# Channel attention on one core: streams of 64 columns, a fourth buffer of rows, and another order on TensorE

## The reference, cut to what matters

```python
q, k, v = xs @ Wq.T, xs @ Wk.T, 2 * (xs @ Wv.T)         # xs: normed rows, 3136 tokens an image, 128 channels
q, k, v_h = l2norm of q, k, v by head                   # 8 heads of 16 channels
attn_head = softmax(einsum('bnhd,bngd->bnhg', v_h, v_h))        # 8 x 8 for each token
q, k = attn_head @ q, attn_head @ k                             # over heads
attn = softmax(einsum('bnhd,bnhe->bnde', k, q))                 # 16 x 16 for each token
out = einsum('bnhd,bnde->bnhe', v, attn)
out = out.transpose(0, 3, 1, 2).reshape(b, n, 128) @ proj_w.T + proj_b   # then x = x + out
```

## Time and profile before

| | |
|---|---|
| median of 3 runs | 3651.51 us (3636.55 to 3661.43) |
| profiled execution | 3654.92 us, its span 3653.1 us |
| TensorE busy, matmuls | 3309.5 us, 91% of the span |
| TensorE busy, weight loads | 2525.6 us, 69% |
| DVE, ACT, POOL busy | 2089.4 (57%), 1480.1 (41%), 246.4 us (7%) |
| mean granted clock of TensorE | 0.90 of the full 2.4 GHz |
| chain that ended last, by engine | PE 20%, DMA 7%, SP's queue 6%, DVE 3%, issue 2%, ACT 1% |
| the attention's part of the span | from 2229 us to the end |

### The profile page before, as it was taken

How to read it: one execution, slowest core, us unless ns; L and a number is a source line. 1 busy time by engine, 2 the same in 40 slices (tenths; PEclk the granted TensorE clock), 3 DMA queues, 4 the chain that set the end, 5 groups by cost and what they waited for, 6 DMA issues and landing times. The chain is left out here.

```text
span 3653.1 us, 106250 instructions
## 1 busy us (share of the span) xinstructions
PE 3309.5 (91%) x44223; PEld 2525.6 (69%) x44223; DVE 2089.4 (57%) x3836; ACT 1480.1 (41%) x3256; POOL 246.4 (7%) x157
## 2 busy tenths in 40 slices
PE   5776978999999999999999895889898989999998
PEld 4553324777777777777777442778787878878787
DVE  4453453666666667666667573445555555455553
ACT  3554412444444444444443443434444444443440
POOL 0000000000000000000000122111111111111110
PEclk9787967999999999999999896879898989898887
DMA  6885004111111221111111993545555555554552
GB/s 149 242 231 144 1 0 156 48 48 49 49 48 48 50 50 49 47 49 49 48 48 45 385 391 108 93 67 105 80 107 92 90 98 89 90 90 93 87 90 42
DMA packets 1033977, 351.34 MB, mean 96 GB/s; under 512 B 888569, under 2 KB 1005991, under 8 KB 1028519
## 3 DMA queue, kind: packets, MB, share of 16 engines
q1 hardware_dynamic: 763952, 251.80, 29.6%
q10 hardware_dynamic: 269687, 94.47, 10.1%
HBM read 174.01 MB, written 172.15 MB: 95 GB/s over the span
## 5 line engine op out<-in xcount | busy, mean ns | idle before, releaser
L751 ACT ACTIVATE x_half<-ps_x 56x228 f32<-56x228 f32 x1024 | 365.1, 357 | 673.4 <-PE ps_x L693 664.3
L801 DVE TENSOR_TENSOR terms<-spec,ps_z 112x456 f32<-112x456 f32 x1024 | 572.8, 621 | 38.0 <-PE ps_z L701 33.1
L708 PEld LDWEIGHTS ps_q<-inv_w,prod 112*114 112x114 f32 x4096 | 434.9, 180 | 27.9 <-issue 25.5
L708 PE MATMUL ps_q<-inv_w,prod 112*114 112x112 f32 x4096 | 451.0, 263 | 1.4 <-DVE prod L805 1.4
L701 PE MATMUL ps_z<-x_half,fwd_w 120*112 120x456 f32 x1024 | 447.0, 559 | 0.8
L811 DVE COPY y_sb<-ps_y 112x224 f32<-112x224 f32 x256 | 100.0, 390 | 414.6 <-PE ps_y L716 331.6
L1126 PE MATMUL ps_s<-v_blocks 128*64 128x64 f32 x6272 | 264.5, 256 | 76.7 <-DMA qk_rows<-qk_heads 72.7
L1126 PEld LDWEIGHTS ps_s<-v_blocks 128*64 128x64 f32 x6272 | 246.5, 169 | 93.2 <-DMA qk_rows<-qk_heads 78.4
L1149 PEld LDWEIGHTS ps_l<-q_mixed,k_blocks 32*64 32x64 f32 x12544 | 232.4, 152 | 91.7 <-issue 75.2
L1100 POOL TENSOR_TENSOR k_blocks<-k_mixed,same_of 128x896 f32<-128x896 f32 x112 | 192.0, 1714 | 1175.2 <-ACT k_mixed L1234 1175.2
L1311 DVE TENSOR_REDUCE z_sum<-p_exp 128x28 f32<-128x448 f32 x112 | 69.4, 620 | 348.1 <-ACT p_exp L1225 348.1
(11 more groups left out here) (120 smaller groups left out, 4699.0 us busy)
## 6 DMA issues: line engine op xcount, KB each, us to landing
conv_in<-v_sb ACTq DMA_DIRECT2D x112, 256.0 KB, 3.3
v_in<-conv_in SPq DMA_DIRECT2D x256, 112.0 KB
qk_heads<-st_qk SPq DMA_DIRECT2D x56, 476.0 KB, 4.2
qk_rows<-qk_heads SPq DMA_DIRECT2D x56, 476.0 KB, 6.9
conv_out<-y_sb ACTq DMA_DIRECT2D x512, 49.0 KB
y<-conv_out SPq DMA_DIRECT2D x8, 1792.0 KB, 13.0
x_in<-in_x SPq DMA_DIRECT2D x8, 1568.0 KB, 9.6
shortcut<-short ACTq DMA_DIRECT2D x8, 1568.0 KB, 6.3
```

What stands on the lines that cost most here:

```text
L708: last = pe.matmul(ps_q[0:2 * NF, c * NFFT:(c + 1) * NFFT], prod[b % 2][:, x, c * 2 * NF:(c + 1) * 2 * NF], k.inv_w[:, x, :], start=(x == ...
L751: last = act.activation(x_half[b % 2][to:to + SIDE, :, a], src, ACT.Copy)
L801: last = dve.tensor_tensor(terms[:, x, :], spec[a][:, s, :], ps_z[b % 2][z][0:NFFT, 0:PC], ALU.mult)
```

## The change: what it does

- The three groups with short streams (`mix` with 33 columns, `logits` and `outputs` with 16) stream 64 columns instead. The extra columns are the following groups' operands, or zeros behind the last; their results fall on columns that the following matmuls write over, or that nobody reads. The number of matmuls, their weights and their order within a group stay.
- `AHEAD` and `NIN` go from 3 to 4: four buffers of `v_blocks` and `qk_rows`. To make room, the residual `x1` has one buffer instead of two.
- The projection alternates between two PSUM buffers; the second is the one that `final` uses. So `final` waits until the projections before it were copied out, and the second projection of a round with a final waits for `add_bias`.
- TensorE's round is scores(i+1), outputs(i-2), mix(i), logits(i-1), final, project, project. ACT's and DVE's rounds follow that order: ACT copies both blocks at the end of its round, DVE adds the bias before it squares.
- The stores of the heads go from SP's queue to ACT's, after `exp_s` of odd rounds. The residual's load goes from SP's queue to ACT's, behind the last store of the image before; that of image 0 to the start.

```diff
-    AHEAD = 3
-    NIN = 3
+    AHEAD = 4
+    NIN = 4
...
-        qk = [sb(f"qk_rows{m}", [128, GB, QKW]) for m in range(NIN)]
+        qk = [sb(f"qk_rows{m}", [128, GB + 1, QKW]) for m in range(NIN)]
-        qm = [sb(f"q_mixed{m}", [128, GU, HD]) for m in range(2)]
+        qm = [sb(f"q_mixed{m}", [128, GU + 3, HD]) for m in range(2)]
-        pn = [sb(f"p_norm{m}", [128, 2, GU, HD]) for m in range(2)]
+        pn = [sb(f"p_norm{m}", [128, 2, GU + 3, HD]) for m in range(2)]
-        x1 = [sb(f"x1_in{m}", [128, TOK]) for m in range(2)]
+        x1 = sb("x1_in", [128, TOK])
-        ps_a, ps_m, ps_o, ps_f = (psum(n) for n in ("ps_qkv", "ps_mix", "ps_o", "ps_fin"))
+        ps_a, ps_m, ps_o, ps_f = (psum(n) for n in ("ps_qkv", "ps_mix", "ps_o", "ps_qkv_fin"))
...  # sync
             def turn(n):
-                sp.wait_ge(st_r, n + 1)
                 at = slice(n * BPB * TB, (n + 1) * BPB * TB)
-                sp.dma_start(t.VT[at]..., st_v[n % 2][:]).then_inc(st_stored[n % 2], 16)
-                sp.dma_start(t.QK[at]..., st_qk[n % 2][:]...).then_inc(st_stored[n % 2], 16)
...
-                if n % NCH == 3:
-                    b = n // NCH
-                    if b > 1:
-                        sp.wait_ge(f_ps, 8 * (b - 1))
-                    sp.dma_start(x1[b % 2][:], t.X1[b]).then_inc(x1_loaded[b % 2], 16)
...  # gpsimd
+                pool.memset(qk[m][:, GB:, :], 0.0)
...  # tensor: project
-                if bk:
-                    pe.wait_ge(qkv_read, bk)
-                pe.matmul(ps_a[0:TB, 0:3 * CH], ...)
+                if bk >= 2:
+                    pe.wait_ge(qkv_read, bk - 1)
+                pe.matmul((ps_f if bk % 2 else ps_a)[0:TB, 0:3 * CH], ...)
...  # mix, logits, outputs
-    last = pe.matmul(ps_m[rows, g * QKM:(g + 1) * QKM], eb[i % 2][rows, g, :], qk[n % NIN][rows, gb, 0:QKM], ...)
+    last = pe.matmul(ps_m[rows, g * QKM:g * QKM + 64], eb[i % 2][rows, g, :], strided(qk[n % NIN][rows], gb * QKW, [[1, 64]]), ...)
-    last = pe.matmul(ps_l[half:half + 64, s // 2, g * HD:(g + 1) * HD], kb[i % 2][rows, g]..., qm[i % 2][rows, g, :], ...)
+    last = pe.matmul(ps_l[half:half + 64, s // 2, g * HD:g * HD + 64], kb[i % 2][rows, g]..., qm[i % 2][rows, g:g + 4, :], ...)
-    last = pe.matmul(ps_o[64 * a:64 * a + 64, g * HD:(g + 1) * HD], vb[n % NIN][:, gb, a, :], pn[i % 2][:, a, g, :], ...)
+    last = pe.matmul(ps_o[64 * a:64 * a + 64, g * HD:g * HD + 64], vb[n % NIN][:, gb, a, :], pn[i % 2][:, a, g:g + 4, :], ...)
...  # final
-                    pe.wait_ge(x1_loaded[b % 2], 16 * (b // 2 + 1))
+                    pe.wait_ge(x1_loaded, 16 * (b + 1))
+                pe.wait_ge(qkv_read, min(NB * BPB, AHEAD * BPB + 2 * (b * UPI + UPI + 3 + u)))
...  # tensor, the round
                 if unit(i + 1):
                     scores(i + 1)
-                if bk < NB * BPB:
-                    project(bk)
+                if unit(i - 2):
+                    outputs(i - 2)
                 if unit(i):
                     mix(i)
-                if unit(i - 2):
-                    outputs(i - 2)
-                if bk < NB * BPB:
-                    project(bk + 1)
                 if unit(i - 1):
                     logits(i - 1)
                 if i in FINS:
                     final(*FINS[i])
+                if bk < NB * BPB:
+                    project(bk)
+                    if i in FINS:
+                        b, u = FINS[i]
+                        pe.wait_ge(f_r, b * 8 + u + 1)
+                    project(bk + 1)
...  # scalar
+            def store_heads(n):
+                at = slice(n * BPB * TB, (n + 1) * BPB * TB)
+                act.wait_ge(st_r, n + 1)
+                act.dma_start(t.VT[at]..., st_v[n % 2][:]).then_inc(st_stored[n % 2], 16)
+                act.dma_start(t.QK[at]..., st_qk[n % 2][:]...).then_inc(st_stored[n % 2], 16)
...  # store(b, u), after the store of the result
+                if u == 7 and b + 1 < BATCH:
+                    act.dma_start(x1[:], t.X1[b + 1]).then_inc(x1_loaded, 16)
+
+            act.dma_start(x1[:], t.X1[0]).then_inc(x1_loaded, 16)
             for bk in range(AHEAD * BPB):
                 copy_in(bk)
-                if bk % BPB == BPB - 1 and bk // BPB + 1 < AHEAD:
-                    root(bk // BPB)
+                if bk % BPB == BPB - 1:
+                    if bk // BPB + 1 < AHEAD:
+                        root(bk // BPB)
+                    if bk // BPB:
+                        store_heads(bk // BPB - 1)
...  # scalar, the round, after root and exp_s(i + 1)
+                if i % 2 == 1 and i // 2 + AHEAD - 1 < NB:
+                    store_heads(i // 2 + AHEAD - 1)
+                if unit(i):
+                    leave_mix(i)
+                if unit(i - 1):
+                    exp_l(i - 1)
                 if bk < NB * BPB:
                     copy_in(bk)
-                if unit(i):
-                    leave_mix(i)
-                if bk < NB * BPB:
                     copy_in(bk + 1)
-                if unit(i - 1):
-                    exp_l(i - 1)
-                if i - 1 in FINS:
-                    store(*FINS[i - 1])
+                if i in FINS:
+                    store(*FINS[i])
...  # vector, the round
+                if unit(i - 2):
+                    leave(i - 2)
                 if unit(i):
                     weigh(i)
-                if unit(i - 2):
-                    leave(i - 2)
                 if unit(i - 1):
                     divide(i - 1)
+                if i in FINS:
+                    add_bias(*FINS[i])
                 pr = AHEAD * 2 + i
...
-                if i in FINS:
-                    add_bias(*FINS[i])
```

More of the change, by code:

```diff
@@ L1035, in attend @@
         in_loaded = [sem(f"in_loaded{m}") for m in range(NIN)]
-        x1_loaded = [sem(f"x1_loaded{m}") for m in range(2)]
+        x1_loaded = sem("x1_loaded")
         out_stored = [sem(f"out_stored{m}") for m in range(4)]
@@ L1062, in turn @@
             def turn(n):
-                sp.wait_ge(st_r, n + 1)
                 at = slice(n * BPB * TB, (n + 1) * BPB * TB)
-                sp.dma_start(t.VT[at].rearrange("(j p) x -> p j x", p=TB), st_v[n % 2][:]).then_inc(st_stored[n % 2], 16)
-                sp.dma_start(t.QK[at].rearrange("(j p) h x -> p j (h x)", p=TB), st_qk[n % 2][:].rearrange("p j h x -> p j (h x)")).then_inc(st_stored[n % 2], 16)
                 m = n % NIN
@@ L1077, in turn @@
                         sp.dma_start(vb[m][64 * a + q:64 * a + 64:4, :, :, at8:at8 + HEADS], v[a, q]).then_inc(in_loaded[m], 16)
-                sp.dma_start(qk[m][:], t.QK[at].rearrange("(g n) h x -> (n h) g x", n=16)).then_inc(in_loaded[m], 16)
+                sp.dma_start(qk[m][:, 0:GB, :], t.QK[at].rearrange("(g n) h x -> (n h) g x", n=16)).then_inc(in_loaded[m], 16)
             for n in range(3):
@@ L1107, in project @@
                     pe.wait_ge(xn_loaded[n % 3], 16 * (n // 3 + 1))
-                if bk:
-                    pe.wait_ge(qkv_read, bk)
-                pe.matmul(ps_a[0:TB, 0:3 * CH], xn[n % 3][:, j * TB:(j + 1) * TB], k.w[:, WQ:WQ + 3, :].rearrange("p a c -> p (a c)"),
+                if bk >= 2:
+                    pe.wait_ge(qkv_read, bk - 1)
+                pe.matmul((ps_f if bk % 2 else ps_a)[0:TB, 0:3 * CH], xn[n % 3][:, j * TB:(j + 1) * TB], k.w[:, WQ:WQ + 3, :].rearrange("p a c -> p (a c)"),
                           start=True, stop=True).then_inc(qkv_ps, 1)
@@ L1137, in mix @@
                         rows = slice(64 * a, 64 * a + 64)
-                        last = pe.matmul(ps_m[rows, g * QKM:(g + 1) * QKM], eb[i % 2][rows, g, :], qk[n % NIN][rows, gb, 0:QKM], start=True, stop=True)
+                        last = pe.matmul(ps_m[rows, g * QKM:g * QKM + 64], eb[i % 2][rows, g, :], strided(qk[n % NIN][rows], gb * QKW, [[1, 64]]), start=True, stop=True)
                 last.then_inc(m_ps, 1)
@@ L1148, in logits @@
                         rows, half = slice(32 * s, 32 * s + 32), 64 * (s % 2)
-                        last = pe.matmul(ps_l[half:half + 64, s // 2, g * HD:(g + 1) * HD], kb[i % 2][rows, g].rearrange("p d m -> p (d m)"), qm[i % 2][rows, g, :],
+                        last = pe.matmul(ps_l[half:half + 64, s // 2, g * HD:g * HD + 64], kb[i % 2][rows, g].rearrange("p d m -> p (d m)"), qm[i % 2][rows, g:g + 4, :],
                                          start=True, stop=True)
@@ L1159, in outputs @@
                     for a in range(2):
-                        last = pe.matmul(ps_o[64 * a:64 * a + 64, g * HD:(g + 1) * HD], vb[n % NIN][:, gb, a, :], pn[i % 2][:, a, g, :], start=True, stop=True)
+                        last = pe.matmul(ps_o[64 * a:64 * a + 64, g * HD:g * HD + 64], vb[n % NIN][:, gb, a, :], pn[i % 2][:, a, g:g + 4, :], start=True, stop=True)
                 last.then_inc(o_ps, 1)
@@ L1173, in final @@
                     at = (e0 + e) * RPI + lo
-                    last = pe.matmul(to, x1[b % 2][:, at:at + RH], k.ident[:], start=False, stop=True)
```

(16 more changed lines are left out.)

## The result

The changed kernel takes 3536.41 us (median of 4 runs, 3527.06 to 3548.5), the kernel before 3649.46 in the same comparison: a ratio of 0.969, 95% interval 0.965 to 0.974. The forecast was 3440, range 3395 to 3580. So the direction is right, and the gain is a little more than half of what I expected: 113 us instead of 210.

A forecast was written before the change was run, and what follows sets the result against it. It took TensorE in the attention as the bound, slowed by a clock of 0.85 and DMA waits; round 1 at 2277, 1122 us for rounds 1 to 111 and a 36 us tail gave 3435, forecast 3440, range 3395 to 3580.

The forecast's parts named there:

- The clock: TensorE in the attention: few streamed columns lower the clock; 64-column streams bring it to 0.97 or more, worth 150 us.
- Rival A: Attention's clock stays as it is, since idle time or something else sets it: 150 us not gained, 3590; chance 0.11.
- the sum: Rounds 1 to 111 of the attention: groups, projections, finals, bias wait, issue gaps and DMA waits add up to 1122 us.
- Logits of 64 columns: Logits on TensorE: four row strips stream at once, paced by weights, 1.78 us a group; bounds 3.36 and 6.7.
- B: Logits: row strips stream in pairs, 3.36 us a group instead of 1.78, at most 3617; chance 0.06.
- C: Logits: row strips do not stream together at all, 6.7 us a group, about 3990, slower than before; chance 0.05.
- Fourth buffer: Waits of scores for qk_rows: a pair's way over DRAM gets 10 us of slack; of 62 us, 5 kept.
- Rival D: A pair's way over DRAM stays the bound: half the DMA waits stay, clock falls in some, 3500 to 3550; chance 0.13.
- The bias: Between the two projections of rounds with a final: new TensorE wait of 0.4 us in 51 rounds, 20 us.
- ACT's wait for the normalized pair: On ACT before the store of a pair: costed at nothing; 1 us in each of 56 rounds would be 56 us.
- The start: Attention's prologue: fewer projections wait for copies and pair 0 is stored sooner; 15 us earlier, between 0 and 25.
- issue gaps as before, 28: TensorE's idle time at issue in rounds 1 to 111: carried over unchanged at 28 us.

The follow-up runs named there:

- e1: Kernel before with only the 64-column streams added (three buffers, old order, one PSUM buffer for the projection): 3587 us.
- e3: Changed kernel with the old streams of 33, 16 and 16 columns, buffers and order as changed: 3674 us.
- e8: Changed kernel with AHEAD and NIN back at 3; streams, order and stores on ACT's queue kept: 3622 us.
- e10: Changed kernel with the stores of the heads back on SP's queue, ahead of the pair's loads: 3542 us.
- e9: Changed kernel without the logits of the third and fourth strip of rows after the first unit: 3409 us.
- e4: Changed kernel without the v_blocks loads for all pairs but the first four, scores working on stale rows: 3465 us.
- e11: e6 with the v_blocks loads left out after the first four pairs: 3420 us.
- e2: Changed kernel with the old rounds on TensorE, ACT and DVE and one PSUM buffer for the projection; streams and four buffers kept: 3549 us.
- e6: Changed kernel with final and first projection ahead of logits, bias before the division, first copy before exp_l: 3500 us.
- e7: e6 with the first projection moved ahead of mix: 3508 us.

## Why the prediction was right, and where it was half as large

**The clock: right in the main.** The step took few streamed columns, not idleness, for what lowers it. The clock rose from 0.86 to 0.98, and e1 and e3 show that it hangs on the columns with either buffering. Rival A is out. Over rounds 1 to 111 TensorE was busy for 1217 us before and 1091 after, so the clock gave 126 of the 150 us that the sum counted on.

"Not idleness" went too far, though. In the changed kernel, nine of the ten falls of the clock between 2300 and 3400 us come right behind a stop of TensorE of 2.3 to 3.1 us. In the timeline above, the stop of 2.42 us before 2410.34 is followed by projections of 1.57 and 1.49 us instead of 0.90 and 0.81. Before that stop and behind it (the third number from the end is the clock):

```profile
2406.00:2409.00 3.00, 1.92 (x115) 1.72 (x111) 0.94 (x3) 0.43 (x2) 1.68 (x1) 1.00 0.70 65
2411.00:2413.00 2.00, 2.00 (x4) 0.62 (x2) 1.57 (x3) 1.04 (x4) 0.00 (x0) 0.50 0.57 132
```

The kernels with wide streams and many DMA waits have the lower clocks among their kind (e1 0.97, e8 0.95). So with narrow streams the clock falls without any stop, and with wide ones what is left of the falls goes with stops. The Trainium skill ("TensorE: Matmul & The Clock Gate", section "Why this matters for your kernels") ties the falls to idle gaps. The falls behind stops agree with it; those with narrow streams do not: in e3 TensorE was busy for 95% of the stretch, before for 92%, and had the lower clock, 0.79 against 0.86.

**Logits of 64 columns: right.** 1.79 us a group where no instruction is missing, against 1.78 forecast and bounds of 3.36 and 6.7. Rivals B and C are out. The Trainium skill, "TensorE: Matmul & The Clock Gate", section "Part 3: Packing small matmuls — row/col tiling", says that matmuls on different strips of 32 rows run at once. The trace agrees, and the group was faster than the 2.2 us that the prediction estimated by the page's figure.

**Fourth buffer: right.** Of 62 us of waits 2.5 were left, in one wait at the start of the stage (5 were kept in the sum). e8 prices the buffer at 86 us. Rival D is out, though the measured time lies in its range of 3500 to 3550 us.

**The bias: right in kind.** 15 us in 41 waits over the stage, against 20 in 51. ACT's wait for the normalized pair cost nothing that e10 can show.

**The start: right.** From the first projection to the scores of round 1 it took 60.0 us before and 48.7 after (2220.03 to 2268.77), 11 us less against 15. The stages ahead of it, which the change doesn't touch, happened to be 12 us shorter in this execution.

**The failed term: "issue gaps as before, 28".** I had carried TensorE's idle time at issue over unchanged, as if it were noise. Rounds 1 to 111 took from 2268.8 to 3492.9 us (the end of the logits before the last but one outputs), 1224 us, against 1122 in the sum: 102 too many. TensorE was busy for 1091 of them, where the sum had 1069 for matmuls at a clock of 1.00, and idle for 133, where the sum had 53 (28 at issue, 20 for the bias, 5 for DMA). The 80 more are issue alone: it took 112 us instead of 28, while the bias and the DMA took less than was set down. In the measure of the table, the gaps grew from 36 to 124 us. The tail took 38.6 us, 36 were forecast.

The sum priced each group by how fast it *ran*, and never asked how fast its instructions *arrived*. The numbers of before would have raised the question: a short round has 112 x 3 + 224 + 8 = 568 instructions of TensorE, some 2.2 blocks of 250, and the trace of before has 210 fetches in 1100 us, one every 5.2 us, where a short round of 8.78 us asks for one every 3.9. They would not have answered it, since they do not say how much faster fetches can come.

The prediction named this outcome among its signs: a clock of 0.97 with a time above 3500 means that a wait costed at nothing carries it. But no rival described that wait. The measured 3536 us lies outside the 3400 to 3490 that the forecast's own chance stood for; the stated range holds it thanks to the room made for D and A, which both did not happen. That part is luck, and so are the 12 us of the start.

Three things together set the new wait: the number of instructions (e9: 112 of 568 fewer, gaps 124 to 24), the DMA traffic of the `v_blocks` loads (e4 and e11: 124 to 68, 102 to 40), and the order on TensorE. The new rounds raised the gaps from 36 to 93 us with three buffers (e1 to e8) and from 89 to 124 with four (e2 to the changed kernel). A mean rate alone does not explain that: e3 and e8 fetch no more often than the kernel before, or hardly so (205 and 212 against 210), and have two and more times its gaps, most of them in the logits, the group with the most instructions per us. That the logits outrun the supply there when they come right behind three other groups is the likely reading, but it is argued. At the higher rate of e6 and e7, moving the final and a projection ahead of the logits took 22 and 18 us of gaps away and left most of them.

**What stays open.** Why fetches come 3.3 us apart at best and 4.7 at the median was not taken apart; when TensorE needs less, as in e9, they also come less often, so a distance is not yet a limit. That they stand behind the loads' small packets is only argued: e4 takes away the loads' bytes, packets and issues at once. A loop over units would need far fewer fetches, as the convolution's does, but wasn't built, since the buffers repeat only after several images; that it would remove the gaps is not shown.

## What to carry to other kernels

When a change speeds up an engine that runs written-out code, count its instructions a round, divide them by the instructions that one block of the trace's instruction queue brings, and compare how often a block is needed with how often one came. Idle time "at issue" inside a group without waits is the sign of that bound; here it grew when the other bounds went. Look at the order too: groups with many short instructions in a row brought such gaps even in slow rounds. Where few columns stream between weight loads and the granted clock is low, wider streams that overwrite each other can cost next to nothing (1.79 us a group of logits instead of 1.75) and bring the clock back. Price a removed wait together with the one behind it: the streams alone brought 54 us, with the DMA wait growing behind them, and with four buffers 138.

## What was not expected of the hardware

- Instructions of written-out code arrive in 16 KB blocks, at best 3.3 us apart, in this stage 4.7 to 5 at the median before the change and after, and in the changed kernel a stop ends 2.2 to 3.0 us after the block's transfer begins. TensorE ran 28,764 matmul instructions with 227 such blocks here, and 7,700 of the looped convolution with 4.
- A matmul instruction of 64 columns on a tile of 32 rows by 64 columns follows the last after 16.0 ns when four tiles take turns (112 in 1.79 us) and after 31.6 ns when two do (56 in 1.77 us).
- At 95% busy TensorE was granted 0.79 of its clock with streams of 16 to 64 columns in the four groups (e3), and at 89% busy 0.98 with streams of 64 (the changed kernel). What was left of the falls there came right behind stops of 2.3 to 3.1 us.
